# Causal mask as 43 more contraction rows in both score products, and the four value-product groups of a step in one block

## The reference

```python
qh, kh = (x @ Wq.T).reshape(B, S, 16, 8), (x @ Wk.T * scale).reshape(B, S, 16, 8)
qk = jnp.einsum('bthd,bshd->bhts', qh, kh)
causal = jnp.tril(jnp.ones((S, S), dtype=bool))
qk = jnp.where(causal, qk, -jnp.inf)
attn = jax.nn.softmax(qk, axis=-1)
vh = v.reshape(B, S, D, H)
qkv = jnp.einsum('bsdh,bhts->bthd', vh, attn)
```

## Time and profile before

| | us |
|---|---|
| median of 3 runs | 657.66 |
| lowest and highest | 656.8, 661.92 |
| the profiled execution's own time | 658.68 |
| its span | 656.9 |
| natural products of steps 0 and 1 | 32.0 to 46.9 |
| attention steps, first score product to last value product | 51.3 to 409.1 |
| expert tiles, first gate product on | 412.2 |

### The profile page before, as it was taken

How to read it: one execution, slowest core, us unless ns; L and a number is a source line. 1 busy time by engine, 2 the same in 40 slices (tenths; PEclk the granted TensorE clock), 3 DMA queues, 4 the chain that set the end, 5 groups by cost and what they waited for, 6 DMA issues and landing times.

```text
span 656.9 us, 15710 instructions
## 1 busy us (share of the span) xinstructions
PE 590.8 (90%) x4889; PEld 405.9 (62%) x4890; DVE 473.6 (72%) x1592; ACT 398.7 (61%) x712; POOL 319.3 (49%) x447
## 2 busy tenths in 40 slices
PE   3789999899999999999999996899988999999940
PEld 1344544445555545555555542899877999999940
DVE  5796767587878869778788784578674766666636
ACT  1205676586786777767876785676544666555612
POOL 4202423245584674855855648345654333333326
PEclk9999999899999999999999998899999999999985
DMA  6643566545335253353262101011232211111138
GB/s 168 205 83 108 176 192 221 138 135 183 86 93 183 59 176 97 99 177 78 78 206 69 50 7 54 23 34 51 63 108 63 59 49 45 44 49 49 42 109 295
DMA packets 64898, 69.05 MB, mean 105 GB/s; under 512 B 8402, under 2 KB 55890, under 8 KB 64834
## 3 DMA queue, kind: packets, MB, share of 16 engines
q1 hardware_dynamic: 59938, 57.16, 30.1%
q0 software_dynamic: 4320, 8.99, 4.4%
q10 hardware_dynamic: 576, 2.10, 0.9%
HBM read 36.92 MB, written 31.03 MB: 103 GB/s over the span
## 4 chain that ended last, share of the span: by engine, by line
PE 74%; DVE 9%; issue 5%; DMA 4%; ACT 3%; POOL 3%; another core or an unknown queue 1%; SPq 0%; ACTq 0%; POOLq 0%; DVEq 0%
PE psN L739 16%; PE psN L491 12%; PE psO L522 11%; PE psT L505 10%; PE psO L750 8%; PE psN L493 4%; PE psM L530 2%; PE psM L552 2%; PE psM L548 1%; DVE negm L1101 1%; DMA kst_all<-k_parts_dram 1%; ACT probs L861 1%; DMA probs<-expert_out 1%; PE psM L595 1%; PE psM L570 1%
## 5 line engine op out<-in xcount | busy, mean ns | idle before, releaser
L1101 DVE TENSOR_REDUCE negm<-psN 128x1 f32<-128x512 f32 (+3 forms) x352 | 215.3, 635 | 60.4 <-PE psN L493 57.4
L861 ACT ACTIVATE probs<-psT 128x512 f32<-128x512 f32 x320 | 185.5, 599 | 67.2 <-PE psT L505 65.4
L491 PE MATMUL psN<-kst_all,qst_all 72*128 72x256 bf16 (+3 forms) x512 | 143.2, 318 | 4.8 <-DMA kst_all<-k_parts_dram 4.3
L739 PE MATMUL psN<-probs 128*128 128x128 f32 x1136 | 140.9, 277 | 2.0 <-ACT probs L978 1.8
L1593 POOL TENSOR_SCALAR_AFFINE_SELECT probs<-probs 128x512 f32<-128x512 f32 x128 | 80.5, 637 | 114.6 <-ACT probs L861 114.0
L739 PEld LDWEIGHTS psN<-probs 128*128 128x128 f32 x1136 | 134.2, 194 | 2.8 <-issue 2.8
L505 PE MATMUL psT<-qst_all,kst_all 74*128 74x384 bf16 (+3 forms) x512 | 124.2, 304 | 2.5 <-ACT probs L861 2.4
L1716 POOL DMA_INDIRECT expert_out<-kst_all,dest x71 | 69.0, 972 | 111.5 <-DVE kst_all L1496 108.2
L493 PE MATMUL psN<-maskts,identb 128*128 128x128 bf16 x512 | 103.7, 228 | 0.0
L491 PEld LDWEIGHTS psN<-kst_all,qst_all 72*128 72x128 bf16 x512 | 51.4, 102 | 81.7 <-DVE negm L1101 39.9
L522 PE MATMUL psO<-probs,vaug 128*32 128x512 f32 (+3 forms) x1024 | 96.7, 449 | 4.2 <-POOL probs L1593 4.1
(11 more groups left out here) (228 smaller groups left out, 698.8 us busy)
## 6 DMA issues: line engine op xcount, KB each, us to landing
q_parts_dram<-qparts SPq DMA_DIRECT2D x24, 384.0 KB, 3.4
k_parts_dram<-kparts SPq DMA_DIRECT2D x24, 384.0 KB, 3.2
qst_all<-q_parts_dram SPq DMA_DIRECT2D x32, 288.0 KB
kst_all<-k_parts_dram SPq DMA_DIRECT2D x32, 288.0 KB
kst_all<-dispatched SPq DMA_DIRECT2D x71, 66.0 KB
xall<-in_x SPq DMA_DIRECT2D x8, 256.0 KB, 4.3
gu_w<-in_gateT SPq DMA_DIRECT2D x4, 512.0 KB, 5.4
gu_w<-in_upT SPq DMA_DIRECT2D x4, 512.0 KB, 5.4
```

The costliest lines, as they stand in the source:

```text
L491: pe.matmul(psN[:, k % NBANKS, col:col + w], qst[g][0:KROWS, j, tb * P:(tb + 1) * P], kst[g][0:KROWS, j, 0:w], start=True, stop=False)
L739: mm = pe.matmul(bank[par][:, c * P:(c + 1) * P], ew[par][:, half, c * P:(c + 1) * P], xgT[par], start=True, stop=True)
L861: nc.scalar.activation(probs[:, g % 2, 512 * u:512 * (u + 1)], psT[:, u % TBANKS, :], ACT.Exp, scale=SOFTMAX_SCALE).then_inc(exp_done, 1)
L1101: nc.vector.tensor_reduce(dst, src, axis=AX.X, op=ALU.max, negate=True).then_inc(nat_done, 1)
```

## The change

Partitions of the stacks are laid out anew: rows 0 and 1 are the maximum rows (ones in kst), rows 2 to 73 the 72 rows of parts, rows 74 to 116 a mask pattern: one row for each three tokens of a 128-token tile. In qst a pattern row holds 2^50, 1 and 2^-50 at its own three tokens and zeros elsewhere; in kst it holds -2^-74, -2^-24 and -2^26 at its own three, -2^76 at all later tokens of the tile and zero at earlier ones. The contraction of these 43 rows gives at least 2^26 in size, negative, where the key is later than the query, and at most 2^-24 in size where it is not.

- Both products contract these rows for the diagonal 128 x 128 piece of a tile only (KMASK = 117 rows), and 74 rows for the rest, so that each tile which is wider than the diagonal piece becomes two products. The natural products contract the two maximum rows too, and a new small DMA sets these rows of qst to zero ahead of each load of the stacks. The `identb` by `maskts` products are gone.
- POOL's four selects per step are gone. The value products wait for the exps alone. POOL's scatters, which stood between the selects, wait for the exps that the selects waited for.
- All four value groups of step s - 1 stand at k = 2 of step s; `keep_values` on ACT moves from k = 6 to k = 4.
- In the set-up POOL makes the two patterns, ACT copies the q pattern into the four qst (64 partitions, 2048 columns each), DVE the k pattern into the four kst in place of the memsets, and SP fills the ones rows by a DMA.

```diff
@@ constants
-MROW = KROWS
-MPARTS = 2
-KALL = KROWS + MPARTS
+KALL = MPARTS + KROWS
+TRIO = 3
+KMASK = KALL + -(-P // TRIO)
@@ SP
             def stacks_in(b, g):
 
+                sp.dma_start(qst[g][0:MPARTS].rearrange("p j (n t) -> p (j n) t", t=P),
+                             zero_b[0:MPARTS].unsqueeze(1).broadcast_to([MPARTS, J * TB, P])).then_inc(st_in[g], 16)
                 for dst, src in ((qst[g], qd), (kst[g], kd)):
-                    sp.dma_start(dst[0:KROWS], src[bass.ds(b * E + g * J * D, J * D)]
+                    sp.dma_start(dst[MPARTS:KALL], src[bass.ds(b * E + g * J * D, J * D)]
...
+            sp.wait_ge(ones_set, 1)
+            sp.dma_start(kst_all[0:MPARTS].rearrange("p g j (n t) -> p (g j n) t", t=P),
+                         ones_b[:].unsqueeze(1).broadcast_to([MPARTS, H * TB, P])).then_inc(ones_in, 16)
@@ PE, nat
                 for col, j, tb, w in nat_blocks(k):
-                    pe.matmul(psN[:, k % NBANKS, col:col + w], qst[g][0:KROWS, j, tb * P:(tb + 1) * P],
-                              kst[g][0:KROWS, j, 0:w], start=True, stop=False)
-                    mm = pe.matmul(psN[:, k % NBANKS, col + w - P:col + w], identb[:], maskts[:],
-                                   start=False, stop=True)
+                    if tb:
+                        pe.matmul(psN[:, k % NBANKS, col:col + w - P], qst[g][0:KALL, j, tb * P:(tb + 1) * P],
+                                  kst[g][0:KALL, j, 0:w - P], start=True, stop=True)
+                    mm = pe.matmul(psN[:, k % NBANKS, col + w - P:col + w], qst[g][0:KMASK, j, tb * P:(tb + 1) * P],
+                                   kst[g][0:KMASK, j, w - P:w], start=True, stop=True)
@@ PE, scores
                 for col, j, blk in exp_blocks(u):
-                    mm = pe.matmul(psT[:, u % TBANKS, col:col + S - P * blk], kst[g][0:KALL, j, blk * P:(blk + 1) * P],
-                                   qst[g][0:KALL, j, blk * P:S], start=True, stop=True)
+                    if blk < TB - 1:
+                        pe.matmul(psT[:, u % TBANKS, col + P:col + S - P * blk], kst[g][0:KALL, j, blk * P:(blk + 1) * P],
+                                  qst[g][0:KALL, j, (blk + 1) * P:S], start=True, stop=True)
+                    mm = pe.matmul(psT[:, u % TBANKS, col:col + P], kst[g][0:KMASK, j, blk * P:(blk + 1) * P],
+                                   qst[g][0:KMASK, j, blk * P:(blk + 1) * P], start=True, stop=True)
@@ PE, values and step
-                pe.wait_ge(masked, 16 * b + 4 * g + c + 1)
                 blk = CHUNKS[c]
-                base, stride, _ = probs_block(blk)
+                base, stride, units = probs_block(blk)
+                pe.wait_ge(exp_done, UNITS * (4 * b + g) + units)
...
-                    if k in (1, 3, 5) and there(b, g, -1):
-                        values(*step_at(b, g, -1), (k + 1) // 2)
-                    if k == 9:
-                        values(b, g, 0)
+                    if k == 2 and there(b, g, -1):
+                        for c in range(TB):
+                            values(*step_at(b, g, -1), c)
@@ ACT
+            def q_pattern(g):
+
+                nc.scalar.activation(qst[g][PAT:P].rearrange("p j (n t) -> p (j n) t", t=P),
+                                     qpat[PAT:P].unsqueeze(1).broadcast_to([P - PAT, J * TB, P]), ACT.Copy
+                                     ).then_inc(qpat_set, 1)
...
-                    if k == 6 and there(b, g, -1):
+                    if k == 4 and there(b, g, -1):
                         keep_values(*step_at(b, g, -1))
@@ DVE
-            def ones_rows(g):
-                V.memset(kst[g][64:96], 1.0).then_inc(consts_ready, 1)
+            def k_pattern(g):
+
+                V.tensor_copy(kst[g][PAT:P].rearrange("p j (n t) -> p (j n) t", t=P),
+                              kpat[PAT:P].unsqueeze(1).broadcast_to([P - PAT, J * TB, P])).then_inc(kpat_set, 1)
@@ POOL
-            def mask(b, g, c):
...
             def scatter_step(b, g, c):
 
                 if g in (2, 3) and has_batch(b - 2):
+                    pool.wait_ge(exp_done, UNITS * (4 * b + g) + probs_block(CHUNKS[c])[2])
                     scatter(b - 2, TB * (g - 2) + c)
```

71 lines of the change are left out of this document (48 added, 23 removed).

## The result

The changed kernel took 686.67 us (median of 6 runs, 681.62 to 692.58), the kernel before 659.39 in the same comparison: ratio 1.040, 95% interval 1.035 to 1.045. It is slower; the forecast was 646.2. A second comparison gave 687.84 against 660.84, ratio 1.044 (1.037 to 1.051). Medians here are of all runs; a ratio and its interval leave out runs that took over 1.5% longer than the kernel's fastest.

The account below looks back on a forecast made before the run. PE's streaming bounds the steady steps; afterwards ACT with two banks would. Gains 1.0 + 1.7 + 1.2 + 1.0 + 2.0 - 0.5 + 5.1 = 11.5 take 658.68 to 647.2, 646.2 as median; range 634 to 659.

Parts of the forecast that it names:

- What bounds the kernel now: Steady steps before the change: bound by what PE streams, PE busy 43.58 of 44.00 us in a batch, ACT with slack.
- Natural and score products: PE's products in each step: natural ones 0.84 us less, cut score products 0.1 us more, the 43 extra contraction rows free.
- The value block: Four value groups at k = 2: 2.5 us (2.3 to 2.7), 2.6 with one hole; PE's pause 3.04 with turn_values.
- ACT's chain through a step: Steady steps: ACT replaces PE as bound, 44.1 us a batch against 44.45, 2.0 gained over steps 5 to 27.
- Set-up: Before the steady steps, step 1's natural products at low clock: about 1.0 us gained; k patterns replacing memsets taken as 0.
- Steps 1 to 4: First steps, by the same chain: 42.5 us against 43.7, 1.2 gained.
- Stacks: Stack loads, mattering in step 6 where PE waits 2.47 us for kst: 1.0 us gained, from 5 gained to 1 lost.
- Steps 28 to 31: Last steps, by the chain, without the batch that isn't there: 0.5 us lost.
- End: Last exp to first gate product: 5.8 us or so instead of 10.85, 5.1 gained, bounds 2 and 6.
- A: Rival: PE stays the bound, steps 1 to 29 keep 1 us each, 38 gained, 620 us; chance 0.12 (A or near it).
- B: Rival: the pause costs more, 6 us lost in the steady steps instead of 2 gained, 654 to 659 us; chance 0.26.
- C: Rival: stacks late in every batch, seven batches pay step 6's wait and low clock, 28 us, 675 in all; chance 0.08.

Follow-up runs that it names:

- natural rows: Kernel before with mask rows in the natural products only, score products, selects and value-group places as before: 661.79 and 658.26 us, ratios 0.995 and 0.994.
- mask rows alone: Changed kernel with value groups back in their four old places and keep_values at k = 6: 649.98 us, ratio 0.988; again 632.72, ratio 0.970.
- shorter exps with the block: Changed kernel, exps of units 3 to 6 taking only 256 of 512 columns from the third step on: 680.83 us, ratio 1.030; again 681.21, 1.031.

## Why the prediction was wrong

**What bounds the kernel now.** Right: PE worked 218.0 of 220.4 us.

**Natural and score products.** Nearly right. By PE's busy time in steps 8 to 27 the natural rows save (218.0 - 204.1) / 20 = 0.70 us a step, I had 0.84; the cut scores cost (208.4 - 204.1) / 20 = 0.21 by the first trace of the mask rows alone and (205.2 - 204.1) / 20 = 0.05 by the second, I had 0.1. A piece with 117 rows starts its successor 0.06 later, as forecast.

**The value block.** 2.29 us at full clock where I took 2.5 and a hole: over-priced, so its length is not the error. At the low level it is 3.17 long.

**ACT's chain through a step.** This is the step that failed, with its sum of 44.1 us per batch; it is a term of the right kind with the wrong size. The mechanism was seen, and most of its signs came: PE works 39.2 of 44 us (38 said), ACT stands 2.06 us behind its third exp, PE waits for exps in the units after the block, the last group ends 3.3 us after the last exp. One sign did not come: ACT's share fell from 32.87 to 29.62 where I had it rise, since ACT did not become full. Steps 8 to 11 of the changed kernel, all at full clock, take 12.4 + 10.9 + 11.6 + 11.6 = 46.5, 2.4 more than the sum. Of this 1.9 stand in g = 2, which I took as PE's own work, 9.65; it took 11.3 and 11.6 at full clock. My upper bound for this term, 45.5, left that out too.

Not all of it is the block. With the mask rows alone g = 2 took 11.2 in the first trace and 10.3 in the second, which has no late exps; some 1 us of the 1.9 is of that kind, which no row of before could show. Against the first trace of the mask rows alone, which has them too, the block adds 0.5 us in g = 0, 0.4 in g = 1, 0.3 in g = 2 and 1.3 in g = 3, 2.5 a batch at full clock. How it does so I can only argue: I followed one chain in each step (ACT's, or PE's in g = 2) and let the others run beside it, while in one PE order with bounded banks they take turns. In step 10 what PE waits for is an exp and then probably a maximum; in the mean it is mostly ACT.

**The clock.** No term had it in the steady steps, though I had read the earlier trace rows, where it falls behind a stall. This is the second thing that failed. At 0.41 us for each low one, 16.9 us make 7 of the 18.6 that separate changed kernel and rows alone in steps 8 to 27 (237.3 - 218.7). The steps with the lengths that they have at full clock give the same: 230.4 us together (step 27 is 9.7, shorter than the others with g = 3), 7 less than 237.3. The rest, some 12 us, is the pause and what follows from it. No run held the clock at 1.00 with the block in.

**The other terms**, from the first exps of the steps before and after. Set-up: 51.92 to 51.29, 0.6 gained for 1.0; step 0: 1.8 for 1.7, right. The k pattern, which I took as a memset, took 1.29 us for two copies, 1.1 less each than the 1.76 of the earlier trace rows; it hardly showed. The Trainium skill's page "VectorE: DVE Perf Modes", section "The TRN2 errata", gives 693 ns for a 2048-column bf16 copy, and the trace agrees with 645. Steps 1 to 4: 45.3 against 43.7, 1.6 lost for 1.2 gained, step 3 at clock 0.87. Stacks: in step 6 PE waited 3.38 us for kst against 2.47, 0.9 lost for 1.0 gained. Steps 5 to 27, with the stacks in them: 274.7 against 256.2, 18.5 lost for 3.0 gained. Steps 28 to 31: 44.6 against 36.7, 7.9 lost for 0.5, two of them at 0.82 and 0.77. End: 3.4 for 5.1. My four parts there add up to 6.1 and not 5.8, and ACT's copy of psO starts at 431.29, 1.06 us after the block's last row ends, late in the sense above. Together 22 us lost; with 0.8 more in the expert tiles that is the 23.0 by which the spans differ.

**The rivals.** A fell: even without the block PE doesn't keep its whole saving; in steps 8 to 27 it stands still for 10.3 and 7.9 us where it stood for 2.4. B was the right direction: it had 6 us lost in the steady steps, where 18.5 were. C did not happen: from 146.6 us to 378 PE waited once for kst, 0.3 us.

## What to carry to other kernels

When an edit puts PE's work into one piece, don't compare the piece with one consumer's buffer only: follow every consumer's chain through the whole step, up to the units that PE must do in order. One chain per step gave 44.1 us here where the kernel took 46.5 at full clock. Where PE was near 100% busy, any edit that gives it idle time can cost clock as well; price both levels (here 0.41 us for each at the low one). Test the halves of a double edit apart: here the good half was 9 us or more, hidden under the other. And where a PE row and the start of its consumer disagree, go by the consumer: the late exps can't be seen in PE's busy time.

## What the runs showed of the hardware

- Less work can bring a lower clock and the same time: shorter exps with the block doubled the time at the low level (16.9 to 34.5 us, and 23.9 to 37.9 in one comparison) and left steps 8 to 27 at 238.6 and 240.9 us, where the changed kernel took 237.3 and 241.3.
- A microsecond at 1.2 GHz cost 0.41 us in these mixed steps, in two kernels (steps 17 and 18 of the changed kernel, step 26 of the natural rows alone).
- 117 contraction rows for a 128-column piece cost no more than 74: 0.06 us from start to start for either (changed kernel, timeline of PE):

```profile
188.44 0.22 PE L507 MATMUL psN<-kst_all,qst_all 74*128 74x128 bf16 x1
188.50 0.22 PE L509 MATMUL psN<-kst_all,qst_all 117*128 117x128 bf16 x1
188.56 0.22 PE L507 MATMUL psN<-kst_all,qst_all 74*128 74x128 bf16 x1
```

- The same kernel stood at 0.988 of before in one comparison (649.98 against 659.13 us) and at 0.970 in another (632.72 against 652.91), intervals far apart: its steps 8 to 27 took 218.7 and 213.1 us, both at a clock of 1.00, the first with 12.0 us of late exps and the second with none. Why they come in some comparisons and not in others, and only with cut score products, I did not find. Small ratios from different comparisons should not be set against each other.
